# Whole-pair transfers for keys, queries and contexts, a gather that adds in SBUF, and a new order of steps

## The reference, cut to what matters

```python
def attention(x, wq, bq, wk, bk, wv, bv, wo, bo, gamma, beta):   # first layer
    Q = (x @ wq + bq).reshape(B * H, S, D)      # H = 16 heads of D = 8: 64 groups of 1024 rows
    K = (x @ wk + bk).reshape(B * H, S, D)      # a plain reshape: a group is 64 rows of x
    V = (x @ wv + bv).reshape(B * H, S, D)
    ctx = softmax(Q @ K^T / sqrt(D)) @ V        # per group, 1024 x 1024 scores
    out = ctx.reshape(B, S, E) @ wo + bo + x
    return layernorm(out) * gamma + beta

x = x + attention(layernorm(x), ...)
x = x + ternary_ffn(layernorm(x), ...)          # 128 -> 512 -> 512 -> 512 -> 128
x = x + gated_linear_attention(layernorm(x), ...)   # per value row a scan over time:
#       h = h * exp(g_t) + k_t * v_t ;  o_t = q_t . h ; then rms norm, gate, output product
x = x + zones(layernorm(x), ...)                # a router picks 3 of 8 experts per batch
```

## Time and profile before

| what | value |
|---|---|
| time, median of 3 runs | 1416.16 us (1413.11 to 1417.28) |
| time of the profiled execution | 1411.4 us |
| its span, first to last instruction | 1409.6 us |
| busy PE, DVE, ACT, POOL | 73%, 49%, 63%, 25% of the span |
| mean busy share of the 16 DMA engines by the main queue | 21.6% |
| bytes read from HBM, written to it | 75.25 MB, 16.78 MB |
| exponentials begin, end | 40.8 us, 1146.5 us |

### The profile page before, as it was taken

The page is one execution under the profiler, slowest core; times in us unless marked ns, Lnnn a source line. Parts: engine busy times, 40 slices in busy tenths (PEclk is TensorE's granted clock), DMA queues, the critical chain, the costliest instruction groups (busy, mean ns, idle before and its releaser), DMA issues.

```text
span 1409.6 us, 16763 instructions
## 1 busy us (share of the span) xinstructions
PE 1034.7 (73%) x5842; PEld 470.4 (33%) x5842; DVE 686.8 (49%) x1235; ACT 885.7 (63%) x1110; POOL 348.6 (25%) x318
## 2 busy tenths in 40 slices
PE   2755588567746956868567977495488789999998
PEld 1211123322223212412233223121152247665666
DVE  3022264053616733656355652763254669979510
ACT  0744579656845955758458876385387876665552
POOL 1000011011302302342223232221132254545300
PEclk7877789878877987998778998797688799999999
DMA  4132112102211222113121221131211123222220
GB/s 106 62 93 78 62 50 61 60 23 69 75 63 40 72 73 69 65 64 79 60 69 53 55 72 65 46 87 56 74 60 58 51 73 97 83 90 98 68 60 16
DMA packets 111423, 93.52 MB, mean 66 GB/s; under 512 B 59184, under 2 KB 82512, under 8 KB 111312
## 3 DMA queue, kind: packets, MB, share of 16 engines
q1 hardware_dynamic: 111168, 92.06, 21.6%
q10 hardware_dynamic: 144, 0.00, 0.0%
HBM read 75.25 MB, written 16.78 MB: 65 GB/s over the span
## 4 chain that ended last, share of the span: by engine, by line
SPq 31%; PE 22%; DMA 16%; DVE 13%; issue 9%; ACT 7%; POOL 3%; ACTq 0%; DVEq 0%; POOLq 0%
SPq L707 15%; DMA R<-VD 10%; SPq L698 6%; PE PS L1466 4%; SPq L682 4%; ACT R L929 4%; PE PS L1626 4%; PE PS L1614 4%; DVE R L1276 3%; PE PS L1443 3%; PE PS L1498 3%; DMA RA<-QD 2%; DVE R L1267 2%; SPq L771 2%; ACT L901 2%
## 5 line engine op out<-in xcount | busy, mean ns | idle before, releaser
L929 ACT ACTIVATE R<-PS 128x1024 f32<-128x1024 f32 x512 | 489.8, 1034 | 248.8 <-PE PS L1443 247.1
L1466 PE MATMUL PS<-R 128*32 128x512 f32 x2048 | 318.4, 669 | 27.4 <-DVE R L1220 27.2
L1443 PE MATMUL PS<-RA 32*128 32x512 f32 x1024 | 186.7, 547 | 137.3 <-DMA RA<-QD 58.3
L882 POOL TENSOR_TENSOR R<-R 128x512 f32<-128x512 f32 x128 | 186.3, 1462 | 301.5 <-ACT R L1004 179.9
L1498 PE MATMUL PS<-RB,WR 128*128 128x512 f32 x640 | 193.3, 443 | 59.0 <-DVE RB L1232 33.4
L1267 DVE TENSOR_TENSOR R<-R 128x512 f32<-128x512 f32 x128 | 103.8, 811 | 262.0 <-DMA R<-VD 257.9
L901 ACT ACT_TABLE_LOAD x136 | 174.5, 1283 | 47.2 <-PE PS L1498 32.1
L1443 PEld LDWEIGHTS PS<-RA 32*128 32x128 f32 x1024 | 72.0, 199 | 380.8 <-ACT R L929 188.1
L1276 DVE TENSOR_TENSOR_SCAN R<-R 128x512 f32<-128x512 f32 x128 | 191.5, 1496 | 2.6
L1498 PEld LDWEIGHTS PS<-RB,WR 128*128 128x128 f32 x640 | 123.5, 202 | 126.9 <-issue 36.1
L868 POOL TENSOR_TENSOR RB<-R,RB 128x512 fp32r<-128x512 f32 x48 | 74.1, 1544 | 278.2 <-DVE RB L1232 257.8
(11 more groups left out here) (121 smaller groups left out, 903.2 us busy)
## 6 DMA issues: line engine op xcount, KB each, us to landing
R<-VD SPq DMA_DIRECT2D x128, 256.0 KB
RA<-QD SPq DMA_DIRECT2D x128, 128.0 KB
QD<-RA SPq DMA_DIRECT2D x128, 64.0 KB, 2.1
RA<-QD SPq DMA_DIRECT2D x256, 32.0 KB
OD<-R SPq DMA_DIRECT2D x128, 32.0 KB, 1.8
R<-OD SPq DMA_DIRECT2D x128, 32.0 KB
R<-in_Wa SPq DMA_DIRECT2D x12, 256.0 KB, 3.5
R<-in_Wb SPq DMA_DIRECT2D x12, 256.0 KB, 4.0
```

The costliest lines, as they stand in the source:

```text
L882: pool.tensor_tensor(st, st, Qc, ALU.mult).then_inc(S["qh"], 1)
L929: act.activation(PR[u % 4], bank(2 * s, 1024), ACT.Exp, scale=SC).then_inc(S["exp"], 1)
L1443: op = pe.matmul(bank(2 * s + h), exact(KS[k][p:p + 32, 128 * j:128 * j + 128]), exact(QS[k][p:p + 32, :]), start=True, stop=not guarded[0])
L1466: op = pe.matmul(bank(ob)[c:c + 32, :], VAF[b % 2][:, at:at + 32], PR[u % 4][:, 512 * h:512 * h + 512], start=(j == 0), stop=(j == 7), til ...
```

## The change

It has four parts.

1. **Queries and keys.** `keep` writes every part twice, so that `QD` holds, for each pair, 64 rows of 1024 numbers for the keys and the same for the queries, already in the order in which the 128 partitions read them. It has four transfers (two parts, two copies) per block for the keys and four for the queries, each with all pairs of the block; in block 0, four for pair 0, four for pair 1 and four for pairs 2 and 3. `keys` and `queries` are one transfer of 128 rows each, whose source patterns begin with a dimension of 2. The columns of the weights `wq` and `wk` are permuted on the host to suit.
2. **Contexts.** `finish` writes the whole tile of 128 x 512 numbers with one transfer. `fetch` has four transfers of 128 rows of 64 numbers, whose source patterns begin with a dimension of 2. The rows of `wo` are permuted to suit.
3. **Gather.** Each of the four gathers of a block is a product of its own in a bank of the common pool; a new DVE step copies the first to the tile `GA` and adds the other three to it. `heads` reads `GA`. Bank 7 joins banks 5 and 6. To make room, `Y2` shares the tile `XN` of its block, so that `norm_in` waits for `x1` where it waited for `y_sum`.
4. **Order.** `ORDER` is a new string with the same count of each letter. At the last letter of the attention (`x`) the old string has 129 steps of the scan (`s`), 40 of the ternary layer (`b`) and 44 of the rest of the scan layer (`t`) still to come, the new one 141, 49 and 48; no step of the experts' products (`d`) stands ahead of it in either.

```diff
-        banks = ((5, 6) if self.acc < 32 else
-                 {"b": (0, 1, 2), "d": (0, 1, 2), "o": (3, 4), "a": (4,), "c": (5, 6)}[who])
+        banks = ((5, 6, 7) if self.acc < 32 else
+                 {"b": (0, 1, 2), "d": (0, 1, 2), "o": (3, 4), "a": (4,), "c": (5, 6, 7)}[who])
...
-        after = [("y_sum", b - 1)] if b >= 2 else []
+        after = [("x1", b - 1)] if b >= 2 else []
...
-                assert self.acc >= LATE
-                self.add("gather", m // 4, m % 4)
+                self.add("gather", m // 4, m % 4, self.take("c"), self.count("gathered"))
...
             def keep(b, w, n0, n1):
                 need.wait_ge("qk_parts", split_no(b, w))
-                for n in range(n0, n1):
-                    for i in range(2):
-                        sp.dma_start(bass.AP(QD.tensor, QD[w, b, n, i, 0, 0:1].offset, [[64, 16], [2048, 8], [1024, 2], [1, 64]]),
-                                     words(Qp[w][:, i, 128 * n:128 * n + 128])).then_inc(S[kept(b, n, w)], 16)
+                for i in range(2):
+                    for copy in range(2):
+                        at = 2 * copy + i if w else 2 * i + copy
+                        sp.dma_start(bass.AP(QD.tensor, QD[w, b, 2 * n0, at, 0, 0:1].offset,
+                                             [[64, 128], [32768, 2 * (n1 - n0)], [1, 64]]),
+                                     words(Qp[w][:, i, 128 * n0:128 * n1])).then_inc(S[kept(b, n0, w)], 16)
...
             def keys(n, k, landed):
-                for h in range(2):
-                    for gg in range(2):
-                        p = 32 * (2 * h + gg)
-                        sp.dma_start(words(KS[k][p:p + 32, :]),
-                                     bass.AP(QD.tensor, QD[1, n // 4, n % 4, 0, 0, 1024 * gg:1024 * gg + 1].offset,
-                                             [[0, 2], [2048, 16], [1, 1024]])).then_inc(S[landed], 16)
+                sp.dma_start(words(KS[k][:, :]), bass.AP(QD.tensor, QD[1, n // 4, 2 * (n % 4), 0, 0, 0:1].offset,
+                                                         [[0, 2], [1024, 64], [1, 1024]])).then_inc(S[landed], 16)
 
             def queries(n, k, landed):
-                for h in range(2):
-                    for gg in range(2):
-                        for i in range(2):
-                            p, at = 32 * (2 * h + gg) + 16 * i, 1024 * gg + 512 * h
-                            sp.dma_start(words(QS[k][p:p + 16, :]),
-                                         bass.AP(QD.tensor, QD[0, n // 4, n % 4, i, 0, at:at + 1].offset,
-                                                 [[0, 2], [2048, 8], [1, 512]])).then_inc(S[landed], 16)
+                sp.dma_start(words(QS[k][:, :]), bass.AP(QD.tensor, QD[0, n // 4, 2 * (n % 4), 0, 0, 0:1].offset,
+                                                         [[512, 2], [1024, 64], [1, 512]])).then_inc(S[landed], 16)
...
             def finish(pr):
...
                 need.wait_ge("ctx_copied", pr + 1)
-                for gg in range(2):
-                    for h in range(2):
-                        c = 32 * (2 * gg + h)
-                        sp.dma_start(bass.AP(OD.tensor, OD[b, q, h, 0, 0, 0, gg, 0:1].offset,
-                                             [[128, 16], [2048, 8], [1, 64]]),
-                                     OS[c:c + 16, :]).then_inc(S["ctx_out"], 16)
+                sp.dma_start(OD[b, q, :, :], OS).then_inc(S["ctx_out"], 16)
...
             def fetch(pr):
...
-                need.wait_ge("ctx_out", 64 * (pr + 1))
+                need.wait_ge("ctx_out", 16 * (pr + 1))
...
-                for h in range(2):
-                    for n, dst in enumerate((CT, DT)):
-                        sp.dma_start(dst[b % 2][64 * h:64 * h + 64, 128 * q:128 * q + 128],
-                                     bass.AP(OD.tensor, OD[b, q, h, 0, n, 0, 0, 0:1].offset,
-                                             [[2048, 8], [128, 8], [1, 128]])).then_inc(S["ctx_in%d" % (b % 2)], 16)
+                for n, dst in enumerate((CT, DT)):
+                    for gg in range(2):
+                        at = 128 * q + 64 * gg
+                        sp.dma_start(dst[b % 2][:, at:at + 64],
+                                     bass.AP(OD.tensor, OD[b, q, 64 * gg + 8 * n, 0:1].offset,
+                                             [[16384, 2], [64, 64], [1, 64]])).then_inc(S["ctx_in%d" % (b % 2)], 16)
...
             def heads(b):
-                act.activation(Oc, bank(7), ACT.Copy, scale=0.125)
-                act.activation(T1, bank(7), ACT.Square, scale=0.25).then_inc(S["heads"], 1)
+                act.activation(Oc, GA, ACT.Copy, scale=0.125)
+                act.activation(T1, GA, ACT.Square, scale=0.25).then_inc(S["heads"], 1)
...
+            def gather(b, q, bk, added):      # on DVE
+                need.wait_ge("gather_ps", 4 * b + q + 1)
+                if q == 0:
+                    if b:
+                        need.wait_ge("heads", b)
+                    dve.tensor_copy(GA, bank(bk)).then_inc(S["gathered"], 1)
+                else:
+                    need.wait_ge("gathered", 4 * b + q)
+                    dve.tensor_tensor(GA, bank(bk), GA, ALU.add).then_inc(S["gathered"], 1)
```

More of the change, by code:

```diff
@@ new lines @@
+    "lxblbbxxbbxbxxbxxxxfxbaxabxxxqxppaxxxxpxaqxxpxraqapxxrprxxslaxrqsxxxsxspfxxqbsxxrsxxxxxxxxsxxsssxbxx"
+    "fxqsssxrslbxsxxxsxxssrbsbxsrbrlxbsxsxbbsxssxxbbblfbsxrxsbsbbsbxssxrsrfsassbbbxrsssbxxxsbrxxbxxsssxax"
+    "bxxbqasxxaxxsxpaapprxpssslxxxxxrssxxpprxsxsxaxsrsxxqfbssxpxqssbxbbfbrrbsbxqbtqxxxrrlxxxxxxxstbxxbbsb"
+    "xsxbssssbsbbqxfxxxxxssssrtxxlrxxxblssssxrsxtxbsbbrxxxsbfsssssxqtsarrssxbxbssxarsxxxxrsxlbssxxtsxasba"
+    "ssxsrsxtrxxxxsxxsxxaxpqpxxxxxprsxfpxqxsapsprsfxxsxssspxssrxxrxqtaxxbxqxxxtxbbxbbbqsrxbssxsxlsxxxlxrs"
@@ L624, in normed_tile @@
         def normed_tile(where, b):
-            return {"X": xblock(b), "XN": XN[b % 2], "Y": Y, "Y2": Y2, "YN": rows4(TT), "YC": YC}[where]
+            return {"X": xblock(b), "XN": XN[b % 2], "Y": Y, "Y2": XN[b % 2], "YN": rows4(TT), "YC": YC}[where]
         def tile(key):
@@ L1170, in residual @@
                 for op, i in ((ALU.mult, 1), (ALU.add, 2)):
-                    own.step(dve.tensor_tensor(Y2, Y2, bc(i), op))
+                    own.step(dve.tensor_tensor(XN[b % 2], XN[b % 2], bc(i), op))
                     own.settle()
-                dve.tensor_tensor(xblock(b), xblock(b), Y2, ALU.add).then_inc(S["x1"], 1)
+                dve.tensor_tensor(xblock(b), xblock(b), XN[b % 2], ALU.add).then_inc(S["x1"], 1)
             def turn(b, bk, e):
@@ L1349, in _ @@
                         down=down, first_c=first_c, decay_2=decay_2,
-                        product=product, state=state, scale_o=scale_o, swish=swish, gate_o=gate_o, add_c=add_c,
+                        product=product, state=state, gather=gather, scale_o=scale_o, swish=swish, gate_o=gate_o, add_c=add_c,
                         pool_x=pool_x, route_2=route_2, route_3=route_3, route_4=route_4,
@@ L1562, in proj_c, with gather @@
                 emptied[bk] = freed
-            def gather(b, q):
-                if q == 0:
-                    room(7)
+            def gather(b, q, bk, added):
+                room(bk)
                 for i in range(4):
@@ L1569, in gather @@
                     need.wait_ge("qh", n + 1)
-                    op = pe.matmul(bank(7)[32 * i:32 * i + 32, :], hot[:, q, :], ST[n % NS], start=(q == 0), stop=(q == 3),
+                    op = pe.matmul(bank(bk)[32 * i:32 * i + 32, :], hot[:, q, :], ST[n % NS], start=True, stop=True,
                                    tile_position=(0, 32 * i))
                 op.then_inc(S["gather_ps"], 1)
-                emptied[7] = ("heads", b + 1)
+                emptied[bk] = added
             def mean_mm(b, bk):
@@ L1678 @@
     cols = lambda s: s.reshape(-1, 128).T
+    turned = lanes % 16 * 8 + lanes // 16
+    gathered = lanes // 64 * 64 + lanes % 8 * 8 + lanes % 64 // 8
     a = {
-        "x": g["L0_attn_x"], "wA": np.stack([g["L0_attn_w" + c] for c in "qkvo"], axis=1),
-        "bA": np.stack([g["L0_attn_bq"], g["L0_attn_bk"]], axis=1),
+        "x": g["L0_attn_x"],
+        "wA": np.stack([g["L0_attn_wq"][:, turned], g["L0_attn_wk"][:, turned], g["L0_attn_wv"], g["L0_attn_wo"][gathered]], axis=1),
+        "bA": np.stack([g["L0_attn_bq"][turned], g["L0_attn_bk"][turned]], axis=1),
         "bv": g["L0_attn_bv"], "bo": g["L0_attn_bo"], "gamma": g["L0_attn_gamma"], "beta": g["L0_attn_beta"],
```

80 lines of the change are left out of this document (37 added, 43 removed).

## The result

The changed kernel takes 1404.9 us in the median (1403.8 to 1409.6, 9 runs) against 1413.8 us for the kernel before (1410.1 to 1419.1, 9 runs beside it): a ratio of 0.9943 with a 95% interval of 0.9924 to 0.9962, faster by 0.6%. The forecast was 1446 us, slower.

A forecast was written before the change was run, and what follows sets the result against it. The prediction took a queue in front of two DMA engines to bound the attention, PE afterwards. Its terms, -7 - 14 + 30 + 0 + 6 + 6 - 12 + 9 + 12 = +30, gave 1446 us; forecast 1420 to 1475, wide range 1375 to 1500.

The forecast's parts named there:

- What bounds the kernel: Attention stretch: a queue in front of two DMA engines, 15.4 us per pair, SP's issues beside it; afterwards PE.
- Loads, keeps and start: Pair loads -7 us (-29 to 0), doubled keeps 0 (-28 to +56), later first load +6 (+3 to +10).
- Contexts out: Context writes: one issue for four saves 1.3 us at 11 places, -14 us (-14 to 0).
- Fetch: Context fetches: 256-byte packets on two engines, 4.4 us each at 11 places, +30 us (+3 to +43).
- the two engines beside the chain: Two DMA engines: 28.8 us of work per pair instead of 23.9, mostly hidden by pauses, +12 us (0 to +61).
- Gather and third bank: DVE additions in SBUF +6 us (0 to +22); fewer PE waits for bank readers -12 (-41 to 0).
- Order: Tail after the attention: 13 us more work where PE is full, less 30% before it, +9 us (0 to +13).
- All 16 engines: Pair loads: destination's 128 rows set the engine count, a load takes 1.9 us; -180 us, 1236 us in all; chance 6%.
- The freed queue pays: SP's queue: issues, not the drain, hold up what follows; faster, 1355 to 1411 us; chance 22%.
- the one sign of being wrong that came true: End of the attention: over before 1130 us would show the forecast wrong.

The follow-up runs named there:

- loads_only: Kernel before with only the doubled keeps and whole-pair loads of keys and queries; contexts and order as before: 1403.6 us, ratio 0.9947.
- contexts_only: Kernel before with only the new context transfers, out by one and fetched by four of 128 rows; old order: 1455.8 us, ratio 1.0330.
- order_reload: Kernel before with the new ORDER string and 27 ACT table loads put back, one in each of pairs 4 to 30: 1391.6 us, ratio 0.9856.
- dma_only: Kernel before with all the new transfers (loads, keeps, contexts) but the old order, gather and banks: 1443.3 us, ratio 1.0249.
- loads_16: Changed kernel with keys and queries each loaded in two transfers of 64 rows, source patterns beginning with 64: 1146.6 us, ratio 0.8143 to the kernel before.
- dma_loads_16: Kernel before with the new transfers, loads cut into two halves of 64 rows; old order and old gather: 1171.9 us, ratio 0.8299.

## Why the prediction was wrong, point by point

**What bounds the kernel: right.** Two engines carry the loads, with 15.4 us per pair; a load alone takes 19 us to the first exponential; the chain stays with loads, replicas and fetches. The Trainium skill, in "DMA: Bandwidth & Descriptors", section "Rules for kernel authors", ties the number of engines to the leading dimension, and the runs agree: 0.13 x 16 = 2.1 engines at 51 GB/s for a leading 2; with a leading 64 a load's stretch shows 0.56 x 16 = 9.0 on the mean at 170 GB/s. The same section says of two transfers of halves "Don't bother" and to use one of 128 partitions. Here the measurement decides against that: two halves in place of one transfer took 255 us off, because the one began with a dimension of 2. The page gives as its reason that both halves spread over all 16 engines anyway; here the one transfer did not.

**Loads, keeps and start: close.** -7 + 0 + 6 forecast, with a share of the +12 besides; -7.5 measured for all of it (loads_only). The terms weren't run one by one; the first load was issued 3.1 us later (24.2 to 21.1 us), where 3.7 was forecast.

**Contexts out: not contradicted**, -14 against about -13, which is the difference of two kernels with unlike fetches.

**Fetch: half of what it costs.** +30 forecast; the runs give +47 for part 2, so about +60 if the write is worth -13; the chain of contexts_only also has about 60 us more of fetches. The price of one was near (4.4 us forecast; 3.5 at the median, up to 6.6 for one of its four transfers). What failed was the number of places: I priced the 11 fetches that stood on the chain, and when fetches grew, more of them came onto it, about 25 of 32 by an estimate (87 us at the median 3.5). Part of this stood in the forecast as "the two engines beside the chain", +12; with that, part 2 was forecast at up to +28 and cost 47.

**Gather and third bank: right.** -12 and +6 forecast, -15 and about nothing measured.

**Order: the step that failed.** +9 forecast, -28 to -30 measured, with the old transfers and with the new. I took an order to be worth what it moves past the last exponential: 13 us more for the last stretch, and 30% of that, 4 us, less for the attention. The moved work was counted about rightly (PE +10.5 us in the last stretch), though the stretch grew by 19.3. What failed is the other side: the attention became 53 us shorter where the term gave it 4. Of what makes up the 53 us, about 10 are table loads (order_reload). PE's waits for loads, which fall by 6.7 us in sum, are not the reason, and 40 of the 53 us come in the last eight pairs, from which the moved work was taken. How much of that is the moved work and how much the better order of what stays is open.

**The sum.** Forecast: +27 for the transfers, -6 for bank and gather, +9 for the order: +30. Measured one upon the other: +35 (dma_only), -28 (order on top of it), -15 (gather and bank on top of that): -8. Of the 38 us between them 37 are the order's; the transfers' 8 too few and the gather's 9 too little gain cancel.

**The rivals.** "All 16 engines" didn't come true for the change, but loads_16 made it, and there its price was too low: loads_16 lies 262 us below the kernel before against the 180 forecast, and with the old order and gather (dma_loads_16) it is still 240. Half of the freed time was to go to other waits; less did, and PE itself was quicker: its granted clock in the attention was 0.93 (loads_16) against 0.83, and it was busy 998 us where the changed kernel has 1040. "The freed queue pays" gave the right sign for a wrong reason: its sign came from the order, while the queue was not freed. So did the one sign of being wrong that came true, the attention over before 1130 us (1119.5).

## What to carry to other kernels

When issues take long, ask first how many DMA engines carry them: a share of 0.13 where only one kind of transfer runs is two of sixteen, and fewer, larger transfers of the same shape only move the wait to the next instruction in the queue. Cut a transfer so that its outermost dimension is large before merging it. And a new order of steps is priced by what the stage loses as well as by what the next one gains, with the waits summed over the whole stage: in part of it they can vanish because they moved to another part.

## What the runs showed of the hardware

**A short write lands late behind a load.** A context write of the changed kernel, 128 rows of 2 KB, in the chain (start us, us, what): it is issued at 534.03, behind a load whose first issue (line 696) is shown before it, from SP in order of time.

```profile
527.69 0.51 SPq L696 DMA_DIRECT2D RA<-QD  x1
...
534.03 15.31 DMA OD<-R
```

It lands at 549.34, 15.3 us after its issue and 21.7 after the load's (527.69). In loads_16 the same write takes 2.1 us at the median (the page there):

```profile
OD<-R SPq DMA_DIRECT2D x32, 256.0 KB, 2.1
```

Its own bytes are a third of the load's. That a part of it lies on the two engines and comes last there would fit both numbers, but isn't shown: the trace has no transfer's packets by engine.

**The holding passes on.** SP takes a load in 1.3 us and is then held 10 us by a replica (554.50 above); behind two loads the four transfers of a fetch hold it 20.6 (407.27). The median issue of a replica is 0.6 us there. So a long issue in these profiles belongs to what is queued ahead of it, and the long issues of queries in the earlier trace rows were no property of queries.

**More engines, faster PE.** With the loads on 16 engines the same products on PE took 4% less busy time (998 to 1040 us) at a mean granted clock of 0.93 instead of 0.83 in the attention. PE's idle time there fell from 341 us (1119.5 less 778.2) to 123 (859.3 less 736.3); that the shorter pauses raised the clock isn't shown.
